# Gathered expert rows in a buffer of their own, added by VectorE, at the end of a two-layer mixture-of-experts and recurrence kernel

## What is computed

```
x = x + 0.5 * ffn(layernorm(x))
x = x + attn(layernorm(x))
x = x + 0.5 * ffn(layernorm(x))

def ffn(x):                        # per token
    shared = (silu(x @ shared_gate.T) * (x @ shared_up.T)) @ shared_down.T
    e      = argmax(x @ gate_w.T)          # one of 8 experts
    xs     = x * sigmoid(max(x @ gate_w.T))
    routed = (silu(xs @ r_gate[e].T) * (xs @ r_up[e].T)) @ r_down[e].T
    return shared + routed
```

## Time and profile before

| what | value |
|---|---|
| median of 3 runs | 900.42 us |
| the three runs | 900.42, 895.29, 900.94 us |
| profiled execution: span from first to last instruction | 896.0 us |
| PE busy, share of the span | 94% |
| last matmul starts | 881.46 us |
| last gather starts on POOL | 885.95 us |

### The profile page before, as it was taken

How to read it: one execution, slowest core, us unless ns; L and a number is a source line. 1 busy time by engine, 2 the same in 40 slices (tenths; PEclk the granted TensorE clock), 3 DMA queues, 4 the chain that set the end, 5 groups by cost and what they waited for, 6 DMA issues and landing times.

```text
span 896.0 us, 16288 instructions
## 1 busy us (share of the span) xinstructions
PE 838.5 (94%) x5398; PEld 729.5 (81%) x5399; DVE 482.5 (54%) x1012; ACT 381.9 (43%) x749; POOL 461.4 (51%) x427
## 2 busy tenths in 40 slices
PE   3999989999999999998898999999999999999993
PEld 2788877888888878887787888888788888888883
DVE  6987553333333336668998886766333333333352
ACT  3353223334333433456677686233243333334230
POOL 5627670333333008869999982676332242230685
PEclk9999999999999999999999999999999999999997
DMA  9795663546464225231111017357344555511565
GB/s 306 260 326 170 204 217 113 183 146 230 156 217 158 95 68 99 41 42 24 30 32 30 24 49 257 120 204 242 124 152 167 187 198 189 189 58 36 106 153 148
DMA packets 72701, 128.76 MB, mean 144 GB/s; under 512 B 6746, under 2 KB 64228, under 8 KB 68292
## 3 DMA queue, kind: packets, MB, share of 16 engines
q0 software_dynamic: 17536, 74.33, 26.8%
q1 hardware_dynamic: 54610, 53.63, 18.8%
q10 hardware_dynamic: 498, 0.02, 0.0%
HBM read 91.64 MB, written 36.32 MB: 143 GB/s over the span
## 4 chain that ended last, share of the span: by engine, by line
PE 65%; POOL 14%; DVE 8%; issue 6%; DMA 5%; ACT 1%; POOLq 0%; ACTq 0%; SPq 0%; DVEq 0%
PE bank L383 19%; PE bank L384 18%; PE bank L385 18%; POOL acc L1789 5%; PE bank L591 4%; POOL xs_sorted L1722 2%; PE bank L560 2%; PE bank L450 2%; POOL v L1694 2%; DVE v L1426 1%; DMA rows<-xn_kept 1%; DMA xs_sorted<-rows,pos 1%; POOL yr L1898 1%; POOL hT_lo L1698 1%; DVE stats L1142 1%
## 5 line engine op out<-in xcount | busy, mean ns | idle before, releaser
L1762 POOL TENSOR_TENSOR wr_lo<-wr_raw,wr_hi 128x3072 fp32r<-128x3072 f32 x14 | 95.2, 6802 | 95.4 <-DMA wr_hi<-w_routed 90.8
L383 PE MATMUL bank<-wr_hi,xT_hi 128*128 x312 | 130.2, 417 | 8.2 <-issue 7.8
L1384 DVE TENSOR_TENSOR hf<-sg,bank 128x512 f32<-128x512 f32 x78 | 53.7, 688 | 133.2 <-PE bank L385 133.2
L384 PE MATMUL bank<-wr_hi,xT_lo 128*128 x312 | 123.7, 397 | 0.0
L385 PE MATMUL bank<-wr_lo,xT_hi 128*128 x312 | 123.1, 394 | 0.0
L1131 DVE TENSOR_TENSOR hT_lo<-bank,hT_hi 128x512 fp32r<-128x512 f32 x78 | 54.0, 692 | 124.4 <-ACT hT_hi L840 124.4
L1789 POOL DMA_INDIRECT acc<-ys_sorted,pos x52 | 87.3, 1680 | 55.3 <-DMA ys_sorted<-rows 40.9
L383 PE MATMUL bank<-xT_hi,ws_hi 128*128 128x512 f32 x256 | 101.9, 398 | 0.4 <-DVE ws_lo L1548 0.4
L384 PE MATMUL bank<-xT_hi,ws_lo 128*128 128x512 f32 x256 | 100.3, 392 | 0.0
L385 PE MATMUL bank<-xT_lo,ws_hi 128*128 128x512 f32 x256 | 100.1, 391 | 0.0
L840 ACT ACTIVATE xT_hi<-bank 128x256 fp32r<-128x256 f32 (+1 forms) x126 | 56.0, 464 | 97.9 <-PE bank L560 87.9
(11 more groups left out here) (234 smaller groups left out, 2117.8 us busy)
## 6 DMA issues: line engine op xcount, KB each, us to landing
wr_raw<-w_routed POOLq DMA_DIRECT2D x16, 1536.0 KB, 7.2
wr_hi<-w_routed POOLq DMA_DIRECT2D x16, 1536.0 KB
rows<-xs_sorted SPq DMA_DIRECT2D x78, 128.0 KB, 2.7
ys_sorted<-rows SPq DMA_DIRECT2D x78, 128.0 KB, 1.8
xn_kept<-xg SPq DMA_DIRECT2D x16, 512.0 KB, 4.5
rows<-xn_kept SPq DMA_DIRECT2D x16, 512.0 KB
xg<-xn_kept SPq DMA_DIRECT2D x12, 512.0 KB
acc<-x SPq DMA_DIRECT2D x8, 512.0 KB, 9.8
```

Of the source, the lines that this page charges most:

```text
L383: pe.matmul(o, a_hi, b_hi, start=start, stop=False, skip_group_check=True)
L384: pe.matmul(o, a_lo, b_hi, start=False, stop=False, skip_group_check=True)
L1384: dve.tensor_tensor(hf[:, 0, :], sg[:, 0, :], MU[:, :], ALU.mult).then_inc(s_mh, 1)
L1762: pool.tensor_tensor(wr_lo[:, e % 2, :], wr_raw[:, :], f32(wr_hi[:, e % 2, :]), ALU.subtract).then_inc(s_wl, 1)
```

## The change

All eight groups are gathered into `yr`, which now has room for 32 tiles. POOL issues 32 plain gathers and no accumulating one, in the order of the shared products: 6, 7, 0, 1, 2, 3, 4, 5. It starts when all slots are done, as before in effect (the wait named is another, and both are met when `y_all_stored` is). DVE adds all eight groups with `add_rows`: four adds in and behind group 4, the second group behind the slots (for groups 6, 7, 0, 1), and four in and behind group 5 (for groups 2, 3, 4, 5). SP stores in the same order, and each store of a whole group waits for DVE's add. The two halves of group 5 are now the last stores.

```diff
-        yr = sb("yr", [P, (NT // GT - NH - 1) * GT, H], F32, final)
+        yr = sb("yr", [P, NT, H], F32, final)
...
-        ADDED = [{}, {3: (LATE[0],)}, {2: (LATE[1],), FB: (LATE[2],)}]
-
-        GATHERED = (6, 7, LATE[0], 0, LATE[1], 1, LATE[2], 2)
-
-        def added(g): return 1 + LATE.index(g)
+        GATHERED = ORDER[1]
+        ADDED = [{}, {0: GATHERED[0:1], 1: GATHERED[1:2], 2: GATHERED[2:3], FB: GATHERED[3:4]},
+                 {0: GATHERED[4:5], 1: GATHERED[5:6], 3: GATHERED[6:7], FB: GATHERED[7:8]}]
+
+        def added(g): return 1 + GATHERED.index(g)
...
-                dve.tensor_tensor(tiles(acc, g), tiles(acc, g), yr[:, bass.ds(LATE.index(g) * GT, GT), :],
+                dve.tensor_tensor(tiles(acc, g), tiles(acc, g), tiles(yr, g),
                                   ALU.add).then_inc(s_fad, 1)
...
-            pool.wait_ge(s_add, 2 * (NG + NH + 1))
+            pool.wait_ge(s_ye, 2 * NS)
             for g in GATHERED:
-                if g not in LATE:
-                    gather(g, s_fin[g])
-                    continue
                 for t in range(GT):
                     pool.indirect_dma_start(
-                        out=yr[:, LATE.index(g) * GT + t, :], out_offset=None, in_=ys_dram,
+                        out=yr[:, g * GT + t, :], out_offset=None, in_=ys_dram,
...
-            for g in GATHERED[:6]:
-                if g in LATE:
-                    sp.wait_ge(s_fad, added(g))
-                else:
-                    sp.wait_ge(s_fin[g], 16 * GT)
+            for g in GATHERED[:-1]:
+                sp.wait_ge(s_fad, added(g))
                 sp.dma_start(tiles(ot, g), tiles(acc, g)).then_inc(s_out, 16)
-            g = LATE[-1]
+            g = GATHERED[-1]
             for a in range(2):
                 first = g * GT + 2 * a
                 sp.wait_ge(s_add, 2 * c_s(1, g) + a + 1)
                 sp.dma_start(ot[:, first:first + 2, :], acc[:, first:first + 2, :]).then_inc(s_out, 16)
-            g = GATHERED[-1]
-            sp.wait_ge(s_fin[g], 16 * GT)
-            sp.dma_start(tiles(ot, g), tiles(acc, g)).then_inc(s_out, 16)
             sp.wait_ge(s_out, 16 * (NG + 1))
```

## The result

The changed kernel took 919.38 us (917.88 to 923.04, four runs). The kernel before took 900.68 on the same chip (895.29 to 901.31, four runs). The ratio is 1.021, with a 95% interval from 1.0174 to 1.0245. The prediction was 893.3 us in a range up to 896.8: wrong in size and in direction.

A forecast was written before the change was run, and what follows sets the result against it. POOL's gathers were taken to bound the last stage. Group 5 landing at 880.7, plus 2.55 on DVE, 2.7 store and 2.9 closing, gave 888.9 against 896.0: 7.1 us off the median, so 893.3 us, range 887.5 to 896.8.

The forecast's parts named there:

- The step that failed: After the slots, the last gather ends up to 14.9 us earlier, but PE's end stays at 881.74 us.
- The slower rival: On POOL, 32 plain gathers in a row take 1.685 us each, not 0.953; 11.3 us slower, 911.7; chance 0.05.
- The gathers: On POOL, 32 plain gathers of 0.953 us with 0.30 us pauses take 39.8 us, plus 5 us of delay.
- Why they are delayed: POOL gathers starting under a DVE instruction with two SBUF inputs wait to about 0.13 us before its end; together 5 us.
- The full lock: Every DVE add holds POOL off for its whole 1.22 us; gain 3.6 us, 896.8; chance 0.16.
- Landing: Rows of a plain gather land 3.1 us after its end, bounds 2.4 and 3.8; group 5 is there at 880.7.
- The adds cost nothing: Five more DVE adds of 1.22 us, 6.1 us in all, fit into DVE's gaps as long as the rows are there.
- the longer PE path: None of the five added adds finds a gap on DVE, PE ends 6.1 us later; gain 1.8, 898.6; chance 0.07.
- The wait foreseen for groups 3 and 4: DVE's adds may wait for late rows: group 3 by 0.6 us; PE's end up to 0.9 later, taken as 0.2.
- DVE's end: Group 5's landing at 880.7 plus 2.55 us for its add through the second shared add: 883.25, later than PE's 882.7.
- The tail: From the last store's issue to the span's end: 2.7 us for the store and 2.9 for the closing, 5.6 together.
- no case gains 9 by itself: No forecast case reaches a gain of 9 us, about 1%, since PE's end allows only 7.8.

The follow-up runs named there:

- x12: The changed kernel itself, unaltered, run as control on another chip, which did not lose: 887.65 us (2 runs), ratio 0.986 to the kernel before.
- after: Profile of one execution of the changed kernel from the first result, with the loss: span 916.3 us, against 896.0 in the profile before.
- x16: The changed kernel with groups 0 and 2 gathered in the old accumulating way, between runs of 8 plain gathers: 894.36 us, ratio 0.993 to the kernel before.
- x8: The changed kernel with each of DVE's eight adds cut to one element of one partition: 892.70 us; the same program took 920.41 on another chip.

## Why the prediction was wrong

**The step that failed.** "That is not the gain, since PE's end at 881.74 is not moved by it." The whole forecast let PE's path depend on the faster gathers only through DVE's adds and the landing of rows. PE's stretch went from 48.9 to 78.5 us, 29.6 more, without either. The sum had no term for what 32 plain gathers in a row do to other engines. The trace of before had none of its kind to read it from: its plain gathers stand in fours, with four at 1.685 us between. The slower rival asked whether the run keeps its own pace, and stopped there; it put the danger on POOL, where there was none.

**Where the chip is free, the steps can be compared with x12**, all from the first gather's start on:

- *The gathers.* Forecast: the last ends after 44.8 us, with 5 us of delay. x12: 43.7 (837.06 to 880.72), so 3.9 us of delay, 1.1 under the forecast and inside its bounds. In `after`, where DVE stood still, 40.1.
- *Why they are delayed.* The gather of 852.37 began under the add of 852.09, which ended at 853.31. It took 1.75, so it lost 0.80, up to 0.14 us before the add's end. That of 866.16 under the add ending at 866.91 lost 0.61, again to 0.14. The full lock (the first rival; the prediction's passage on the ports calls it the second) would have cost 8.5 us, and the gathers lost 3.9 in all. The adds themselves kept 1.22 to 1.26.
- *Landing.* Forecast 3.1 us behind the gather's end. Measured 883.55 - 880.72 = 2.8.
- *The adds cost nothing.* PE's stretch is 48.9 with them, as before; the longer PE path (rival two) did not come. The only wait for rows is 1.45 us, for group 5. The wait foreseen for groups 3 and 4 did not show.
- *DVE's end.* Forecast 883.25 - 832.83 = 50.4. Measured 886.68 - 837.06 = 49.6. PE sets it, with 0.49 us of idle before the last shared add, while the forecast had the landing of group 5 set it.
- *The tail.* Forecast 5.6 us from there to the end of the span, 2.7 for the store and 2.9 for the closing. Measured 889.6 - 886.68 = 2.9 in x12 and 916.3 - 913.71 = 2.6 in `after`. The store took 2.2, and the closing behind SP's last branch was no constant: 0.7 us in x12 against 2.9 before, and 1.9 in x16. What it waits for stands beside SP's branch:

```profile
L72 POOLq DRAIN  x1: 24708/24708/24708, 864.6 to 864.6; - x1
...
L72 SPq COMPARE_BRANCH  x1: 37/37/37, 888.9 to 888.9; - x1
```

The closing DRAIN of POOL's queue runs from 864.6 to 889.3, 8.6 us past the end of POOL's last gather. In all twenty traces of this case it ends 8.0 to 9.6 us after that gather, and the span ends 0.2 to 0.3 us behind the DRAIN or 0.3 to 0.4 us behind SP's branch, whichever is later. In the kernel before it ended at 866.3 + 29.5 = 895.8, so POOL's last gather set the end of the span at 896.0, and the store of group 2, over at 893.1, did not. The prediction put this down as a fixed closing of 2.9 us behind SP, a term that was mis-sized because it belongs to POOL. An estimate with its own last gather at 877.6: 877.6 + 8.3 + 0.2 = 886.1 by POOL, 883.3 + 2.7 + 0.4 = 886.4 by SP, so a gain of 9.6 us and not 7.1. The sentence that no case gains 9 by itself falls with it.

The span of x12 (889.6) being so near the forecast's 888.9 is in part luck: its first gather starts 4.2 us later, which about undoes the 2.7 us of the tail and the 0.8 of DVE. The gain in the runs there, 901.26 to 887.65, was 13.6 us and not 7.1; with two runs at 891.37 and 883.92 that is a loose number.

So the steps for POOL's gathers and DVE's adds were right and closely sized, the closing was put on the wrong engine, and the hold on PE, DVE and ACT was missing. The hold was worth four times all that the forecast had in it.

## What to carry to other kernels

Look at what a change makes longer in a row than anything in the trace before: a run of 32 indirect gathers at 1.26 us starved PE, ACT and DVE in the first result and on two of four chips later, and runs of 8 with slower gathers or a wait between them did not, on the one losing chip where they ran. Where an engine sits idle for "remote" or "issue" though its input was ready, look for what another engine does at that time and not for a wait of its own. And compare kernels on several chips with a control on each: one chip gave this change 0.986, another 1.027, and the cut-down x8 would have convicted the wrong cause. The mixed order x16 (0.993 on the chip where the change cost 2.7%) is the version to keep; it was not run on a free chip. And where POOL issues the last gathers, count its DRAIN of 8 to 9 us behind them as a path to the end of its own: it still set the end of x12 and x16.

## What had not been expected of the hardware

- PE, ACT and DVE together slowed to steps of 0.70 us or stood still, from 13 us after the first of the gathers to 5 us after the end of the last, with the DMA engines at 36% and 105 GB/s. On a losing chip PE's stretch was 78.5, 79.9 and 79.4 us for one program, on a free one 48.9: two levels with nothing between for this kernel.
- The loss is smaller when the gathers are thinned: at 1.43 us a gather it cost 14 us (64.9 against 50.8), PE was full for 20 us, and then it waited for DVE and ACT, which were held from about 14 us on.
- POOL's closing DRAIN ended 8.0 to 9.6 us after its last gather in every trace, and in the kernel before it set the end of the span.
- A gather of POOL that starts while DVE runs an instruction with both inputs in SBUF is held to 0.14 us before that instruction's end; one that runs already is not held. In x12 the gather of 878.52 was not held either: it began 0.01 us after the add of 878.51, took 0.94, and the add took 1.26.
